# Two depthwise convolutions on TensorE: a ring of channel-outermost copies in front of the band products

## What is computed

```python
x = x + dwconv(x, pos_w, pos_b)                       # 3x3, one filter per channel
q, k, v = proj(layernorm(x, ln1_g, ln1_b))
x = x + out_proj(attention(q, k, v) + dwconv(v, lepe_w, lepe_b))   # 5x5, one filter per channel
return x + mlp(layernorm(x, ln2_g, ln2_b))
```

## Time and profile before

| | |
|---|---|
| runs without profile | 2617.33, 2617.39, 2621.17 us; median 2617.39 |
| profiled execution | 2628.1 us, its span 2626.3 us |
| mean granted TensorE clock | 0.912 of full speed |
| PE, DVE, ACT, POOL busy | 84%, 57%, 47%, 40% of the span |
| pos phase | 0 to about 372 us of the span |
| lepe phase | about 1896 to 2186 us |

### The profile page before, as it was taken

How to read it: one execution, slowest core, us unless ns; L and a number is a source line. 1 busy time by engine, 2 the same in 40 slices (tenths; PEclk the granted TensorE clock), 3 DMA queues, 4 the chain that set the end, 5 groups by cost and what they waited for, 6 DMA issues and landing times. The chain is left out here.

```text
span 2626.3 us, 85046 instructions
## 1 busy us (share of the span) xinstructions
PE 2196.2 (84%) x31886; PEld 1742.7 (66%) x31886; DVE 1490.1 (57%) x2350; ACT 1238.4 (47%) x2079; POOL 1061.6 (40%) x1661
## 2 busy tenths in 40 slices
PE   6977515988888898897898989989779984999998
PEld 6977513656666666665666666666579983777777
DVE  3677874656556565554565666666431213677675
ACT  2444531534444444453454544444334554666665
POOL 2344554434444344433444444444312233433433
PEclk9988755989989999887998999999889996999999
DMA  6575536665666666667666666666396753444442
GB/s 106 114 173 154 154 113 143 154 133 132 140 141 143 147 135 143 141 146 166 147 153 146 148 150 149 157 150 161 69 142 124 159 128 101 96 96 94 95 95 68
DMA packets 716326, 348.34 MB, mean 133 GB/s; under 512 B 613481, under 2 KB 675137, under 8 KB 716097
## 3 DMA queue, kind: packets, MB, share of 16 engines
q1 hardware_dynamic: 686993, 314.26, 53.7%
q0 software_dynamic: 28800, 30.58, 4.0%
q10 hardware_dynamic: 304, 0.03, 0.0%
HBM read 105.39 MB, written 102.76 MB: 79 GB/s over the span
## 5 line engine op out<-in xcount | busy, mean ns | idle before, releaser
L693 ACT ACTIVATE att_prob<-att_st_ps 128x448 f32<-128x448 f32 x896 | 487.2, 544 | 674.4 <-PE att_st_ps L585 673.0
L768 DVE TENSOR_REDUCE att_mm<-att_s_ps 128x8 f32<-128x448 f32 x896 | 548.6, 621 | 263.0 <-PE att_s_ps L552 262.0
L598 PEld LDWEIGHTS att_pv_ps<-att_vx,att_prob 128*56 128x56 f32 x14336 | 543.6, 137 | 141.4 <-issue 18.6
L598 PE MATMUL att_pv_ps<-att_vx,att_prob 128*56 128x18 f32 x14336 | 510.8, 205 | 1.8 <-ACT att_prob L693 1.8
L580 PE MATMUL att_st_ps<-att_mvt,att_both 122*56 122x448 bf16 x1792 | 341.0, 376 | 161.9 <-DMA att_mvt<-att_mneg 116.3
L552 PE MATMUL att_s_ps<-att_kx,att_q_unit 120*56 120x448 bf16 x1792 | 335.9, 371 | 5.7 <-DMA att_q_unit<-att_qk_hi 3.2
L585 PE MATMUL att_st_ps<-att_qx,att_k_hi 128*56 128x448 bf16 x1792 | 339.6, 374 | 0.0
L585 PE MATMUL att_st_ps<-att_qx,att_k_lo 128*56 128x448 bf16 x1792 | 336.6, 371 | 0.0
L430 POOL COPY att_vx<-att_vf 56x224 f32<-56x224 f32 x512 | 182.0, 386 | 306.8 <-PE att_pv_ps L598 298.3
L445 POOL DMA_DIRECT2D att_mvt<-att_mneg x256 | 135.8, 535 | 307.8 <-PE att_st_ps L585 232.6
L436 POOL DMA_DIRECT2D att_qx<-att_q_hilo x512 | 245.0, 487 | 26.9 <-DMA att_q_hilo<-att_qk_lo 15.8
(11 more groups left out here) (207 smaller groups left out, 3283.3 us busy)
## 6 DMA issues: line engine op xcount, KB each, us to landing
att_xt<-xn_chunks SPq DMA_DIRECT2D x128, 196.0 KB, 3.6
att_k_hi<-att_qk_hi SPq DMA_DIRECT2D x128, 196.0 KB, 3.8
att_k_lo<-att_qk_lo SPq DMA_DIRECT2D x128, 196.0 KB, 4.1
att_qx<-att_q_hilo POOLq DMA_DIRECT2D x512, 49.0 KB, 3.0
pos_x<-in_x_dram SPq DMA_DIRECT2D x128, 105.0 KB, 3.6
lepe_x<-v_scratch SPq DMA_DIRECT2D x128, 105.0 KB, 3.0
x_scratch<-pos_x SPq DMA_DIRECT2D x128, 98.0 KB
xn_chunks<-pos_xrt SPq DMA_DIRECT2D x16, 784.0 KB, 4.9
```

Source lines behind the costliest of these rows:

```text
L598: ins = pe.matmul(pv_ps[v % 2][64 * h:64 * h + L, at:at + 18], prob[t % 4][:, 4 * h + a, :], vx[v][:, VW * j + 36 * a + 18 * h:VW * j + 36 ...
L693: act.activation(prob[t % 4][:, :, :], st_ps[t % 2][:, 0:S8].rearrange("p (s q) -> p s q", q=L), ACT.Exp).then_inc(exp_done, 1)
L768: dve.tensor_reduce(mm[v % 2][:, NH * j:NH * j + NH], s_ps[j % 2][:, 0:S8].rearrange("p (s k) -> p s k", k=L), AX.X, ALU.max).then_inc(max ...
```

## The change

A ring `xg` of 8 buffers `[128, 4 channels, 8, 15 rows]` in f32 (15 rows: JB + 1) is added. A new function `relay` copies four channels of all four images of a batch from X into it, with the channel outermost and the rows contiguous: 480 elements a partition. The products read `xg`. Who copies: POOL in pos and for batch 0 of lepe, DVE for the other batches of lepe. In pos the factor 1/C of the variance goes into the square's scale, -1/C of the mean into one `scalar_tensor_tensor`, and EPS is added on POOL. In SP's order `load` comes ahead of `store_t`, and takes the place of image n instead of image n-1. `rezero(n)` now comes after the power of n, ahead of the copies for image n+1.

```diff
+        def relay(eng, b, cg, done):
+            t = 16 * b + cg
+            if cg == 0:
+                eng.wait_ge(framed, b % 2 + 1)
+                eng.wait_ge(x_in[b % 2], 128 * NB4 * (b // 2 + 1))
+                if b >= 2:
+                    eng.wait_ge(rezeroed, NB4 * (b - 1))
+            if t >= RING:
+                eng.wait_ge(conv_done, t - RING + 1)
+            eng.tensor_copy(xg[t % RING][:, :, :, :].rearrange("p c n j -> p c (n j)"),
+                            X[b % 2][:, :, :, :, 4 * cg:4 * cg + 4].rearrange("p n s j c -> p c (n s j)")).then_inc(done, 1)
...
# SP, for each image n
+                if b + 2 < NBATCH:
+                    load(b + 2, q)
                 if n >= LAG:
                     store_t(n - LAG)
-                if n and images[n - 1][0] + 2 < NBATCH:
-                    load(images[n - 1][0] + 2, images[n - 1][1])
...
# POOL
+            def ahead(n):
+                if n < len(images) and images[n][0] + 1 < NBATCH:
+                    for cg in range(4):
+                        relay(pool, images[n][0] + 1, 4 * images[n][1] + cg, relaid)
+            for cg in range(16):
+                relay(pool, 0, cg, relaid)
+            if pos:
+                ahead(0)
             for n, (b, q) in enumerate(images):
                 if pos:
                     if n:
-                        rezero(n - 1)
                         lo(n - 1)
-                    pool.wait_ge(var_sb, n + 1)
-                    pool.tensor_tensor(st[u][:, 3, :], st[u][:, 2, :], half[:, :], ALU.pow).then_inc(rs_done, 1)
+                    pool.wait_ge(var_in, n + 1)
+                    pool.tensor_scalar(st[u][:, 1, :], st[u][:, 1, :], EPS, None, ALU.add).then_inc(eps_done, 1)
+                    pool.wait_ge(eps_done, n + 1)
+                    pool.tensor_tensor(st[u][:, 2, :], st[u][:, 1, :], half[:, :], ALU.pow).then_inc(rs_done, 1)
+                    rezero(n)
+                    ahead(n + 1)
...
# PE, conv(b, cg)
+                if pos or b == 0:
+                    pe.wait_ge(relaid, t + 1)
+                else:
+                    pe.wait_ge(relaid_dve, t - 15)
...
-                                        X[u][:, :, :, d:d + JB, c].rearrange("p n s j c -> p (n s) j"),
+                                        xg[t % RING][:, k, :, d:d + JB],
...
# ACT
-                    act.activation(sq[:, :, :], xc[n % 2][:, :, :], ACT.Square).then_inc(sq_done, 1)
+                    act.activation(sq[:, :, :], xc[n % 2][:, :, :], ACT.Square, scale=C ** -0.5).then_inc(sq_done, 1)
...
# DVE, center(n) and variance(n)
-                dve.tensor_scalar(st[u][:, 1, :], st[u][:, 0, :], -1.0 / C, None, ALU.mult).then_inc(mean_sb, 1)
...
-                dve.tensor_tensor(blocks(xc[u][:, :, :]), x1, mean, ALU.add).then_inc(xc_done, 1)
+                dve.scalar_tensor_tensor(blocks(xc[u][:, :, :]), total, -1.0 / C, x1, ALU.mult, ALU.add).then_inc(xc_done, 1)
...
-                dve.tensor_scalar(st[u][:, 2, :], st[u][:, 0, :], 1.0 / C, EPS, ALU.mult, ALU.add).then_inc(var_sb, 1)
...
# DVE, lepe
+            if not pos:
+                for cg in range(4):
+                    relay(dve, 1, cg, relaid_dve)
+                add_attention(0)
...
-                else:
-                    add_attention(n)
+                elif n + 1 < B:
+                    add_attention(n + 1)
+                    b1, q1 = images[n + 1]
+                    if b1 + 1 < NBATCH:
+                        for cg in range(4):
+                            relay(dve, b1 + 1, 4 * q1 + cg, relaid_dve)
```

More of the change, by code:

```diff
@@ L912, in conv_phase @@
     D = 2 * R + 1
+    RING = 8
     with ExitStack() as ctx:
@@ L917, in conv_phase @@
         X = [sb(f"x{u}", [128, NB4, 2, JB + 1, C], F32) for u in range(2)]
+        xg = [sb(f"xg{u}", [128, 4, 2 * NB4, JB + 1], F32) for u in range(RING)]
         hl = [sb(f"hl{u}", [128, NBLK, 2 * C], BF16) for u in range(2)]
@@ L923, in conv_phase @@
             xct = sb("xct", [128, W, H], BF16)
-            st = [sb(f"st{u}", [128, 4, NBLK], F32) for u in range(2)]
+            st = [sb(f"st{u}", [128, 3, NBLK], F32) for u in range(2)]
             half = sb("half", [128, NBLK], F32)
@@ L954, in conv_phase @@
         id_done = sem("id_done")
+        relaid, relaid_dve = sem("relaid"), sem("relaid_dve")
         conv_done = sem("conv_done")
@@ L958, in conv_phase @@
         xr_sb, xc_sb = sem("xr_sb"), sem("xc_sb")
-        mean_in, mean_sb, xc_done = sem("mean_in"), sem("mean_sb"), sem("xc_done")
-        sq_done, var_in, var_sb, rs_done = sem("sq_done"), sem("var_in"), sem("var_sb"), sem("rs_done")
+        mean_in, xc_done = sem("mean_in"), sem("xc_done")
+        sq_done, var_in, rs_done = sem("sq_done"), sem("var_in"), sem("rs_done")
+        eps_done = sem("eps_done")
         xn_done, hi_done, lo_done = sem("xn_done"), sem("hi_done"), sem("lo_done")
@@ L1284, in center @@
                 dve.wait_ge(mean_in, n + 1)
-                dve.tensor_scalar(st[u][:, 1, :], st[u][:, 0, :], -1.0 / C, None, ALU.mult).then_inc(mean_sb, 1)
-                dve.wait_ge(mean_sb, n + 1)
                 if n >= 2:
@@ L1289, in center @@
                     dve.wait_ge(hi_done, n - 1)
-                mean = st[u][:, 1, :].rearrange("p (s j) -> p s j", s=2).unsqueeze(3).to_broadcast([128, 2, JB, C])
-                dve.tensor_tensor(blocks(xc[u][:, :, :]), x1, mean, ALU.add).then_inc(xc_done, 1)
+                total = st[u][:, 0, :].rearrange("p (s j) -> p s j", s=2).unsqueeze(3).to_broadcast([128, 2, JB, C])
+                dve.scalar_tensor_tensor(blocks(xc[u][:, :, :]), total, -1.0 / C, x1, ALU.mult, ALU.add).then_inc(xc_done, 1)
             def variance(n):
@@ L1295, in variance @@
                 dve.wait_ge(sq_done, n + 1)
-                dve.tensor_reduce(st[u][:, 0, :], sq[:, :, :], AX.X, ALU.add).then_inc(var_in, 1)
-                dve.wait_ge(var_in, n + 1)
-                dve.tensor_scalar(st[u][:, 2, :], st[u][:, 0, :], 1.0 / C, EPS, ALU.mult, ALU.add).then_inc(var_sb, 1)
+                dve.tensor_reduce(st[u][:, 1, :], sq[:, :, :], AX.X, ALU.add).then_inc(var_in, 1)
             def scale(n):
@@ L1303, in scale @@
                 dve.tensor_tensor(xc[u][:, :, :], xc[u][:, :, :],
-                                  st[u][:, 3, :].unsqueeze(2).to_broadcast([128, NBLK, C]), ALU.mult).then_inc(xn_done, 1)
+                                  st[u][:, 2, :].unsqueeze(2).to_broadcast([128, NBLK, C]), ALU.mult).then_inc(xn_done, 1)
             def col_copy(n, halves):
```

2 lines of the change are left out of this document (removed).

## The result

The changed kernel takes 2606.6 us (median of 20 runs, 2596.5 to 2617.7) against 2623.9 for the kernel before (20 runs, 2611.6 to 2640.7): a ratio of 0.9932, interval 0.9911 to 0.9953. Faster, by 17 us; 113 were forecast, and the time is outside the range. The profiled execution is the longest of the 20, 2617.7 us with a span of 2615.9.

What follows compares the result with a forecast made beforehand. PE was taken to bound the convolution stretches, load holes and a DVE-bound tail the rest of pos. 58 us off in pos and 55 in lepe, taken from 2617.4, gave 2504 us; range 2445 to 2550.

Steps and rivals of the forecast that it cites:

- Part 1: Convolution products on PE read the ring: a record 0.125 us instead of 0.204, a group 2.2 us instead of 3.26.
- rival C: Convolution products on PE: a record stays at 0.204 us, the stride not being the cost; 2597 us in all; chance 0.07.
- Part 2: Ring copies on POOL and DVE: 0.83 us each; batch 0 gets 17 us shorter in pos and 17 in lepe.
- rival D: Ring copies: strided copy far dearer, slower overall from 3.2 us a copy, 2684 us at 4 us; chance 0.05.
- Part 3: New order in pos: SP's turn 13.05, then 17 us; last write-back at 240.5 instead of 291.0, 50.5 us off including batch 0's 17.
- Rival A: Pos: landings are quick, SP keeps up, POOL's 12.1 us an image bounds; 2476 us in all; chance 0.20.
- Rival B: Pos and lepe: copies and DVE's two-input operations keep each other waiting, 27 us more, 2531 us; chance 0.17.
- Part 4: Folded scalings in the tail of pos, where DVE is the bound: 1.9 us an image for four images, 7.5 us.
- Part 5: Lepe, batches 1 to 3: loads wait for no store, 133.6 us instead of 172, 38 us off.
- As the change doesn't touch the other phases: Attention and MLP: no difference, so the 113.4 us are taken off the median of 2617.4.

Runs made afterwards that it cites:

- e7: Changed kernel, but in pos POOL's four ring copies of an image wait for DVE's multiplication of that image: 2605.9 us, 0.9956 of the kernel before.
- e10: Changed kernel with store ahead of load, two `xct` buffers, 202 more PE waits, and half of pos's ring copies (batches 1 to 3) on ACT: 2516.2 us, 0.9594.
- e16: Kernel before with the folded scalings alone (EPS added on POOL): 2616.1 us, 0.9987 of the kernel before.
- e8: Changed kernel with SP's order of the kernel before (store of image n-3, then load of image n-1): 2592.2 us, 0.9893 of the kernel before.
- e1: Kernel before with PE's later instructions shifted by 54 through satisfied waits, to place 1382: 2655.4 us, 1.0138 of the kernel before.

## Why the prediction was wrong

- **Part 1 held**, and batch 0 with it: 67.9 us against 68.6. So rival C falls. There was luck in the size: 0.109 us times both factors, 1.14 and 1.17, is 0.145, and the 0.125 that I wrote has only one of them. The record cost 0.11. It holds at the full clock alone; at a clock of 0.50 a group costs 3.59 us with the ring as without it.
- **Part 2 held roughly**: POOL's copies start 0.95 us apart (0.83 forecast), DVE's take 0.71 in the median. So rival D falls.
- **Part 3 failed, and it is the step that failed first.** I had SP's turn as a sum: store issues, landing, load issues, transfers, 13.05 and 17 us. The landing, priced at 3.6 us, took 1.9 to 2.1 for images 0 to 2 (from the end of the store's issues to the load), and then it was hardly the wait: the loads of images 3, 5, 6 and 7 go within 0.03 us of the end of the centering that they wait for, that of image 4 one us behind it. I wrote that `store_t(n-3)` is queued behind the load's wait, and priced its bytes, but did not ask who waits for that store. DVE does, and through the centering so does the next load: a loop. The turns came at 16.5 to 18 us (images 0 to 2, the multiplication held off by the copies) and 20.3 to 22.0. The last write-back is at 274.4 us in place of 240.5 forecast: 34 of the 42 us missed in pos. Rival A, that SP keeps up, falls with it.
- **Rival B** (0.17) had its mechanism right, 3.7 us a multiplication (e7, and half of it in e10), but beside the loop, not in place of it.
- **Part 4 failed whole**, 7.5 us: "in the tail DVE is the bound" is true only while nothing else is within 1.9 us of it, and the loop through POOL's power was within 0.6: e16 has the folded scalings alone, its turns fall from 13.3 to 12.7 us, and pos stays at 373.5.
- **Part 5** forecast 133.6 us for batches 1 to 3; they took 155.7, again by the store behind the load, on which ACT's row copy waits; with the old order lepe is 16 us shorter (e8). Batch 0, from lepe's start, took 66.2 us in place of 87.7: 21 gained, 17 forecast.
- **"As the change doesn't touch the other phases"** was wrong by 36 us (e1), the time that PE loses in attention at place 1382 against 1328. No row of the profile before showed what PE's place is worth; it did show the 3.96 us on issue once an image and 194 instruction packets, and I read neither.

The sum: 113 forecast, less 42 in pos, 17 in lepe and 36 to 44 in attention, leaves 10 to 18; measured 17. The 36 is e1's, the 44 the one profiled execution's.

## What to carry to other kernels

When a transfer is moved past another on a queue, ask for each one who waits for its landing, and follow that waiter to the queue's next wait; if it closes a loop, the turn is the sum of the loop, not of the queue. A change that alters the number of instructions ahead of a long loop on PE moves that loop: look at the instruction queue's packets, at idle times on "issue" and at the duration of the loop's branch, and try the kernel at another place before judging the change. When an engine's work is removed, look how far behind the next one is; here it was 0.6 us.

## What the chip showed that I had not expected

- The place of PE's loop is worth up to 120 us of some 2600: 2655.4, 2623.9 and 2535.2 us for one and the same kernel with 54, 0 and 128 more idle instructions. The branch at its end takes 4.4 us (0 more) and 0.21 us (128 more).
- A group of f32 products whose columns lie 16 bytes apart costs as much as one with 256 (3.45 and 3.26 us), and 1.96 if they are adjacent. At half the clock the last two are alike, 3.59 us for the 16 records.
- Four copies of POOL back to back, 3.8 us, hold a waiting two-input operation of DVE for all four; it does not get in between them (5.76 us in place of 2.02). With two copies ahead of it, it takes 3.87.
